# Graph layers on one core: GpSimd's wait for a turn's sums, from group 5 on instead of from group 2 on

## Chip, core and metric

One core of a Trainium2 chip. The metric is the device time of one execution in microseconds, the median of several runs.

## What is computed

12,500 nodes of 32 features, 400,000 edges sorted by destination. Two layers, each followed by a residual and a normalisation:

```python
m = relu(x[src] + edge_attr)
neigh = segment_sum(m, dst)
x = layernorm(x + (1 + eps) * x + neigh)
# second layer
h = x * rsqrt(clip(out_degree, 1))
agg = segment_sum(h[src], dst)
x = layernorm(x + agg * rsqrt(clip(in_degree, 1)))
```

## The kernel before

The edges are cut into 125 groups of 3200 (128 partitions by 25 edges). The first phase, `layer_0`, goes through them in turns, and each engine runs its own program of `step(g, slot, u)`; they meet only in semaphores. `turns` (line 227) writes out g = 0 to 3, runs g = 4 to 119 in a hardware loop of 29 passes by four slots (there `g` is an expression of the loop's register, not a Python integer), and writes out g = 120 to 126.

In turn g these things happen:

- GpSimd (lines 567 to 579) gathers the source nodes' rows of group g from DRAM into `rows`, slot g % 4, by 25 indirect DMAs (`gathers`, line 160), each for 128 edges. Ahead of them it waits for the group's indices (`z_in`), from group 4 on for VectorE's additions of group g - 4 out of the same slot (`z_sum[1]` at g - 3), and for `z_agg` at g - 1.
- VectorE (`step`, line 416) works on the rows of group g - 1: it adds them to the edges' features (`add`, line 426, in two halves; the first waits for all 25 gathers), takes further steps on the sums (`left`, line 431, `last_part`, line 435), and makes one-hot matrices of indices (line 143 records them all). It also makes one-hot matrices (`chunk`) from which TensorE builds, in `built`, counts for the second phase.
- ScalarE copies edge features into the bank (`copy`, line 599), applies the Relu (`first_part`, line 606) and evicts the counts to `stage` (line 621). Its order is written out by hand: the eviction of the first piece stands between `copy(0)` and `first_part(0)`.
- TensorE builds the counts (line 687, 24 matmuls a turn) and sums group g - 1's messages in 25 matmuls (line 667), three each between the last built pieces and 19 at the end. The last one raises `z_agg` to g; "sum g" below is that. So the sum of turn g is that of group g - 1.
- SyncE (line 537) loads, every second turn, the indices and edge features of groups g + 2 and g + 3, behind waits for `z_copy[1]` and `z_idx[3]` at g; it stores each turn's counts to `stash` (line 548). The indices and features of groups 0 to 3 are loaded at the beginning.

After the last turn come `finish_0` (normalisation), `layer_1`, which has no gathers and is TensorE's, and `finish_1`. They follow each other in blocks. `s_mark` is a semaphore that is raised behind waits and that no one waits for.

Of the kernel before, what the change touches and what calls it, by code (L numbers as in the profile page):

```python
# [16 lines left out]
def build(nc, x, src, dst, edge, eps, out, table, x1):  # L17
# [47 lines left out]
    with ExitStack() as ctx:  # L65
# [94 lines left out]
        def gathers(gp, j0, j1, nodes, rows_d, src_d, s):  # L160

            for j in range(j0, j1):
                gp.indirect_dma_start(  # L163
                    rows_d[:, j, :], None, nodes,
                    bass.IndirectOffsetOnAxis(ap=src_d[:, j:j + 1].bitcast(U32), axis=0),
                ).then_inc(s, 16)
# [54 lines left out]
        def layer_0():  # L221
# [5 lines left out]
            def turns(engine, step):  # L227
                for g in range(4):
                    step(g, g, 0)
                with engine.Fori(0, fours) as i:  # L230
                    for slot in range(4):
                        step(i * 4 + (4 + slot), slot, i + 1)
                for g in range(4 + 4 * fours, G + 2):
                    step(g, g % 4, g // 4)

            def builds(g):

                return not isinstance(g, int) or g < G
# [13 lines left out]
            def loaded(engine, s, s_first, slot, use, n):  # L252

                if isinstance(use, int) and use == 1 and slot == 0:
                    engine.wait_ge(s_first, n)
                else:
                    engine.wait_ge(s[slot // 2], use * n)

            with ExitStack() as own:
# [137 lines left out]
                with nc.Block() as block:  # L397
# [163 lines left out]
                    @block.gpsimd  # L561
                    def _(gp):

                        for h in range(2):
                            gp.iota(pick_i[:, h, :], [[1, max(HT)], [0, SPAN]], base=h * HT[0], channel_multiplier=0).then_inc(s_const, 1)

                        def step(g, slot, u):
                            if builds(g):
                                loaded(gp, z_in, z_in0, slot, u + 1, IN)
                                gp.sem_inc(s_mark, 1)  # L570
                                if not isinstance(g, int) or g >= 4:

                                    gp.wait_ge(z_sum[1], g - 3)
                                    gp.sem_inc(s_mark, 1)
                                if not isinstance(g, int) or g >= 2:

                                    gp.wait_ge(z_agg, g - 1)
                                    gp.sem_inc(s_mark, 1)
                                gathers(gp, 0, J, x[:, :], rows[:, slot, :, :], src_t[:, slot, :], z_rows[slot])
                        turns(gp, step)  # L580
# [739 lines left out]
```

## Time and profile before

| | us |
|---|---|
| median of 3 runs (5220.22 to 5222.47) | 5221.61 |
| profiled execution | 5230.44 |
| its span | 5228.60 |
| first phase, to the last gather's start | 3948.04 |
| granted TensorE clock, mean over the span | 0.731 |

```profile
span 5228.6 us, 62768 instructions
...
PE   4555555555555555555555555555555999999997
PEld 1111111111111111111111111111113888888886
DVE  6666666666666666666666666666665444444445
ACT  4555555555555555555555555555554555555553
POOL 6777777777777777777777777777771000000000
```

The digits are the busy share of each engine (PE is TensorE, PEld its weight loads, DVE VectorE, ACT ScalarE, POOL GpSimd) in tenths, in 40 equal slices of the span. The first 30 slices are the first phase, in which POOL is busy, the last nine the second, in which TensorE is. Times below are microseconds from the start of the span.

### The profile page before, as it was taken

Reading aid. Unit: us, or ns where it says so; the run is one execution under the profiler, and the core shown is the slowest. Engines: PE = TensorE matmul, PEld = TensorE weight load, DVE = VectorE, ACT = ScalarE, POOL = GpSimd, SP = SyncE. Lnnn points to the kernel's source line nnn. Section 1 sums busy time; section 2 is a strip of 40 time slices with the busy share of each in tenths; the row PEclk is TensorE's granted clock in tenths of the full one; section 3 lists DMA queues with packets and bytes.
Section 4 is the critical chain, followed back from the end, with each engine's and each line's share of the span. In section 5 each row is a group of like instructions: output and inputs, shape, how many; then the busy total and the mean of one; then the engine's idle time right before and its main releaser. Section 6 shows DMA issues by size and latency. Waiting matters only on the chain. (4 is left out here: it accounts for less than half of the span.)

```text
span 5228.6 us, 62768 instructions
## 1 busy us (share of the span) xinstructions
PE 3323.6 (64%) x21148; PEld 1679.4 (32%) x21148; DVE 3288.0 (63%) x4730; ACT 2760.6 (53%) x2908; POOL 2969.7 (57%) x3134
## 2 busy tenths in 40 slices
PE   4555555555555555555555555555555999999997
PEld 1111111111111111111111111111113888888886
DVE  6666666666666666666666666666665444444445
ACT  4555555555555555555555555555554555555553
POOL 6777777777777777777777777777771000000000
PEclk7666666666666666666666666666666999999998
DMA  3333333333333333333333333333334999999995
GB/s 123 119 119 119 119 130 130 119 119 119 127 133 125 119 119 119 124 136 119 119 119 125 130 130 119 119 119 122 135 119 146 325 324 325 324 325 326 323 324 207
DMA packets 269134, 867.71 MB, mean 166 GB/s; under 512 B 90218, under 2 KB 140218, under 8 KB 252602
## 3 DMA queue, kind: packets, MB, share of 16 engines
q1 hardware_dynamic: 169107, 815.98, 42.1%
q0 software_dynamic: 100000, 51.40, 6.6%
q8 instruction: 13, 0.21, 0.0%
q14 instruction: 14, 0.11, 0.0%
HBM read 486.77 MB, written 380.38 MB: 166 GB/s over the span
## 5 line engine op out<-in xcount | busy, mean ns | idle before, releaser
L163 POOL DMA_INDIRECT rows<-in_x,src_t x3125 | 2968.1, 950 | 976.0 <-issue 946.5
L687 PE MATMUL built<-x_parts,b_hot 100*128 100x490 bf16 x3000 | 1294.1, 535 | 1774.2 <-ACT big L621 1759.8
L621 ACT ACTIVATE big<-built 128x980 bf16<-128x980 f32 x1500 | 1804.4, 1229 | 551.3 <-PE built L687 548.4
L687 PEld LDWEIGHTS built<-x_parts,b_hot 100*128 100x128 bf16 x3000 | 250.1, 111 | 2664.8 <-ACT big L621 2041.7
L426 DVE TENSOR_TENSOR sum_ps<-sum_ps,rows 128x416 f32<-128x416 f32 x250 | 143.0, 572 | 1246.7 <-DMA rows<-in_x,src_t 1242.1
L870 PE MATMUL applied<-counts,x_parts 128*96 128x160 bf16 x12250 | 916.1, 233 | 1.4 <-ACT counts L828 1.4
L667 PE MATMUL agg<-hot,msg 128*128 128x512 bf16 x3125 | 907.2, 441 | 4.9 <-DVE msg L456 4.9
L870 PEld LDWEIGHTS applied<-counts,x_parts 128*96 128x96 bf16 x12250 | 880.2, 123 | 64.9 <-ACT counts L828 2.3
L143 DVE TENSOR_TENSOR x_parts<-iota_ps,hk_g 100x3920 bf16<-100x3920 f16 x375 | 819.6, 2186 | 0.0
L828 ACT ACTIVATE counts<-built 128x980 bf16<-128x980 f32 x500 | 598.8, 1238 | 391.1 <-PE built L856 391.0
L143 DVE TENSOR_TENSOR hot<-iota_ps,s_hi 128x5252 bf16<-128x5252 f16 x250 | 691.4, 2765 | 0.0
L606 ACT ACTIVATE msg<-sum_ps 128x416 bf16<-128x416 f32 x250 | 123.0, 492 | 810.2 <-DVE sum_ps L426 810.2
L667 PEld LDWEIGHTS agg<-hot,msg 128*128 128x128 bf16 x3125 | 352.4, 113 | 510.1 <-issue 248.8
L610 ACT ACTIVATE msg<-sum_ps 128x416 bf16<-128x416 f32 x250 | 126.0, 504 | 387.1 <-DVE sum_ps L431 387.1
L856 PE MATMUL built<-big,hi_hot 100*128 100x490 bf16 x1000 | 273.1, 374 | 33.4 <-DVE big L143 27.8
L143 DVE TENSOR_TENSOR big<-iota_ps,hk_g 100x3920 bf16<-100x3920 f16 x125 | 273.7, 2190 | 0.0
L794 DVE CAST slots<-small 80x64 bf16<-80x64 f32 x125 | 27.6, 221 | 373.0 <-PE small L881 373.0
L143 DVE TENSOR_TENSOR b_hot<-iota_ps,hk_g 100x1024 bf16<-100x1024 f16 x375 | 255.2, 681 | 7.9 <-PE built L687 3.6
L143 DVE TENSOR_TENSOR hot<-iota_ps,rel 128x1404 bf16<-128x1404 f16 x250 | 209.7, 839 | 0.0
L810 DVE TENSOR_TENSOR acc<-acc,small 32x128 f32 x125 | 34.5, 276 | 206.8 <-PE small L891 206.8
L599 ACT ACTIVATE sum_ps<-edge_t 128x416 f32<-128x416 f32 x250 | 127.0, 508 | 67.9 <-DVE msg L435 67.9
L431 DVE SCALAR_TENSOR_TENSOR sum_ps<-sum_ps,msg 128x416 f32<-128x416 f32 x250 | 141.8, 567 | 1.7 <-ACT msg L606 1.7
(130 smaller groups left out, 1452.2 us busy)
## 6 DMA issues: line engine op xcount, KB each, us to landing
stash<-big SPq DMA_DIRECT2D x125, 2940.0 KB, 9.1
counts<-stash SPq DMA_DIRECT2D x250, 1470.0 KB, 8.6
rows<-in_x,src_t POOLq DMA_INDIRECT x3125
edge_t<-in_edge_attr SPq DMA_DIRECT2D x61, 800.0 KB
big<-in_dst SPq DMA_DIRECT2D x1, 1562.5 KB
big<-in_src SPq DMA_DIRECT2D x1, 1562.5 KB
src_t<-in_src SPq DMA_DIRECT2D x61, 24.8 KB
dst_t<-in_dst SPq DMA_DIRECT2D x61, 24.8 KB
```

Of the source, the lines that this page charges most:

```text
L143: return ve.tensor_tensor(out.rearrange("p n (w t) -> p n w t", t=2), row[0:p, 0:w].rearrange("p (w t) -> p w t", t=2).unsqueeze(1).to_bro ...
L163: gp.indirect_dma_start(rows_d[:, j, :], None, nodes, bass.IndirectOffsetOnAxis(ap=src_d[:, j:j + 1].bitcast(U32), axis=0),).then_inc(s, 16)
L426: ve.tensor_tensor(half(h), half(h), rows[:, prev, j0:j1, :], ALU.add).then_inc(z_sum[h], 1)
L431: ve.scalar_tensor_tensor(half(h), half(h), 0.0, part(0, h), ALU.max, ALU.subtract).then_inc(z_left[h], 1)
L599: sc.activation(half(h), edge_t[:, prev, j0:j1, :], ACT.Copy).then_inc(z_copy[h], 1)
L610: sc.activation(part(1, h), half(h), ACT.Copy).then_inc(z_part1[h], 1)
L621: sc.activation(stage[:, slot % 2, q, :, d0:d0 + 2 * SPAN].rearrange("p c (b d) -> p b c d", b=2), built[n % 2][:, :, 0:KEYS].rearrange("p ...
L667: last = te.matmul(agg_bank[:, :], msg[:, j, :], hot[:, j, :], start=(j == 0), stop=(j == J - 1))
L687: last = te.matmul(built[n % 2][:, b, 0:KEYS], b_hot[:, r, t, :], key_hot[:, r, t, :], start=True, stop=True)
L828: sc.activation(counts[:, slot, HB, :, d0:d0 + 2 * SPAN].rearrange("p c (b d) -> p b c d", b=2), built[n % 2][:, :, 0:KEYS].rearrange("p b ...
L856: last = te.matmul(built[n % 2][:, b, 0:KEYS], hi_hot[:, slot, t, :], key_hot[:, slot, t, :], start=True, stop=True)
L870: last = te.matmul(applied[slot].rearrange("m (q d) -> m q d", d=CS), x_parts[:, c, :], counts[:, other, :, c, :], start=(c == 0), stop=(c ...
```

## The change

GpSimd's wait for `z_agg` gets another condition. Where `g` is a Python integer it was there from 2 on and is now there from 5 on. Where `g` belongs to the hardware loop (groups 4 to 119) the condition's first half holds in both versions.

```diff
@@ -572,7 +572,7 @@
                                     gp.wait_ge(z_sum[1], g - 3)
                                     gp.sem_inc(s_mark, 1)
-                                if not isinstance(g, int) or g >= 2:
+                                if not isinstance(g, int) or g >= 5:
 
                                     gp.wait_ge(z_agg, g - 1)
                                     gp.sem_inc(s_mark, 1)
```

## Rows read from the trace of the kernel before

**Rows 1.** The page: busy time of the engines, two of the costliest groups.

```profile
PE 3323.6 (64%) x21148; PEld 1679.4 (32%) x21148; DVE 3288.0 (63%) x4730; ACT 2760.6 (53%) x2908; POOL 2969.7 (57%) x3134
...
L163 POOL DMA_INDIRECT rows<-in_x,src_t x3125 | 2968.1, 950 | 976.0 <-issue 946.5
...
L426 DVE TENSOR_TENSOR sum_ps<-sum_ps,rows 128x416 f32<-128x416 f32 x250 | 143.0, 572 | 1246.7 <-DMA rows<-in_x,src_t 1242.1
```

**Rows 2.** Waits of POOL: total us, times, longest us.

```profile
POOL rows L163 <- issue: 946.5, 3104, 0.3
POOL rows L163 <- PE agg L667: 24.9, 20, 19.1
POOL rows L163 <- DMA dst_t<-in_dst: 4.6, 1, 4.6
```

**Rows 3.** Timeline of POOL: start, duration, instruction, [idle before <- releaser].

```profile
81.17 0.95 POOL L163 DMA_INDIRECT rows<-in_x,src_t  x1 [0.30 <-issue]
101.22 0.95 POOL L163 DMA_INDIRECT rows<-in_x,src_t  x1 [19.10 <-PE agg L667]
...
131.24 0.94 POOL L163 DMA_INDIRECT rows<-in_x,src_t  x1 [0.30 <-issue]
132.49 0.95 POOL L163 DMA_INDIRECT rows<-in_x,src_t  x1 [0.30 <-issue]
...
163.76 0.95 POOL L163 DMA_INDIRECT rows<-in_x,src_t  x1 [0.30 <-issue]
...
195.12 0.95 POOL L163 DMA_INDIRECT rows<-in_x,src_t  x1 [0.31 <-issue]
...
3948.04 0.94 POOL L163 DMA_INDIRECT rows<-in_x,src_t  x1 [0.30 <-issue]
```

**Rows 4.** Line 163, whole span, then 101.2 to 1101.2: ns min/median/max.

```profile
L163 POOL DMA_INDIRECT rows<-in_x,src_t x3125: 943/947/3924, 9.5 to 3948.0; - x196
...
L163 POOL DMA_INDIRECT rows<-in_x,src_t x800: 943/947/1031, 101.2 to 1101.0; - x160
```

**Rows 5.** Timeline of PE: the closing 19 matmuls of sums 1 to 4.

```profile
96.14 4.27 PE L667 MATMUL agg<-hot,msg 128*128 128x512 bf16 x19
...
119.08 4.73 PE L667 MATMUL agg<-hot,msg 128*128 128x512 bf16 x19
...
153.18 4.74 PE L667 MATMUL agg<-hot,msg 128*128 128x512 bf16 x19
...
184.65 4.37 PE L667 MATMUL agg<-hot,msg 128*128 128x512 bf16 x19
```

**Rows 6.** Timeline of DVE: turn 2, turn 3 and the start of turn 4.

```profile
98.13 0.60 DVE L426 TENSOR_TENSOR sum_ps<-sum_ps,rows 128x416 f32<-128x416 f32 x1 [1.02 <-ACT sum_ps L599]
...
102.56 0.60 DVE L431 SCALAR_TENSOR_TENSOR sum_ps<-sum_ps,msg 128x416 f32<-128x416 f32 x1 [1.13 <-ACT msg L606]
...
133.58 0.60 DVE L426 TENSOR_TENSOR sum_ps<-sum_ps,rows 128x416 f32<-128x416 f32 x1 [12.99 <-DMA rows<-in_x,src_t]
...
136.79 0.59 DVE L431 SCALAR_TENSOR_TENSOR sum_ps<-sum_ps,msg 128x416 f32<-128x416 f32 x1
...
165.05 0.60 DVE L426 TENSOR_TENSOR sum_ps<-sum_ps,rows 128x416 f32<-128x416 f32 x1 [10.35 <-DMA rows<-in_x,src_t]
```

**Rows 7.** Timeline of ACT: the copy ahead of turn 3's addition.

```profile
120.47 0.53 ACT L599 ACTIVATE sum_ps<-edge_t 128x416 f32<-128x416 f32 x1
```

**Rows 8.** Timeline before the first turn: two gathers, a VectorE instruction.

```profile
23.46 3.18 POOL L163 DMA_INDIRECT rows<-in_x,src_t  x1 [0.30 <-issue]
...
37.99 3.49 DVE L352 SCALAR_TENSOR_TENSOR big<-x_parts,big 125x3200 f32<-125x3200 f32 x1
...
38.38 3.92 POOL L163 DMA_INDIRECT rows<-in_x,src_t  x1 [0.30 <-issue]
```

**Rows 9.** Timeline of SP's queue: last index load for groups 4 and 5.

```profile
113.58 0.56 SPq L519 DMA_DIRECT2D dst_t<-in_dst  x1
```

**Rows 10.** Timeline of DVE: the last group's first addition.

```profile
3951.02 0.60 DVE L426 TENSOR_TENSOR sum_ps<-sum_ps,rows 128x416 f32<-128x416 f32 x1 [13.24 <-DMA rows<-in_x,src_t]
```

## The prediction

> **What bounds the kernel now.** Read the page first, and its table of engines last. No engine has over 64% of the span, and the page's chain of waits stops after the last microseconds, so neither names the bound. The lines of the costliest groups do [rows 1]: in the first phase VectorE idles 1242.1 us ahead of its additions and was released by the landing of gathered rows, while GpSimd's 976.0 us of idle time is spread over 3125 gathers. The waits view splits that [rows 2]: 946.5 us in 3104 pieces of at most 0.3 us, which end on nothing that the profile shows (the price of starting one gather), and only 24.9 us that ended on TensorE's sums, one piece of them 19.1 us. So in the first phase GpSimd issues gathers one behind another and everything else follows it. One gather costs 1.2508 us from start to start: (131.24 - 101.22) / 24 inside group 2 [rows 3]. A group of 25 costs 31.27 us, which is the distance from group 2's first gather to group 3's, 132.49 - 101.22, and from 3 to 4, 163.76 - 132.49. From group 2 to the end it is the same: (3948.04 - 101.22) / 3074 = 1.2514 us. VectorE takes up the last group's rows 3 us behind the last gather [rows 10], and the rest of the program comes after that in order. What GpSimd gains in the first phase and isn't made to wait for again, the program gains.
>
> **What is removed.** The wait before group g's gathers asks for g - 1 sums. In the diff its start moves from group 2 to group 5, but groups 4 to 119 run in a hardware loop in which g is no Python integer, and there the condition is true in both versions. So exactly two waits go (with one marker increment each), of groups 2 and 3; group 4 keeps its own, for 3 sums. The other waits of groups 2 and 3 (their indices) were met long ago: the indices were among the loads of the beginning.
>
> Group 2. Group 1's last gather starts at 81.17, group 2's first at 101.22 after 19.10 us of idle time [rows 3]; a normal gap is 0.30. Saved: 19.10 - 0.30 = **18.80 us**. New start: 81.17 + 1.25 = 82.42.
>
> Group 3. It followed group 2 without a gap, since sum 2 had come at 119.08 + 4.73 = 123.81 [rows 5], before 132.49. In the new order it starts at 82.42 + 31.27 = 113.69, and now its removed wait matters: kept, it would hold until 123.81 plus the 0.81 us that passed from the end of sum 1 (96.14 + 4.27 = 100.41) to 101.22, so 124.62. Removed, it costs nothing.
>
> The other 19 releases by TensorE in the waits view hold 24.9 - 19.1 = 5.8 us, 0.3 each, the normal gap: nothing is to be had there, and nothing was lost.
>
> **What is next late: group 4.** Its gathers could start at 113.69 + 31.27 = 144.96, if sum 3 is there. Before, sum 3 ended at 153.18 + 4.74 = 157.92 [rows 5], because turn 3 had to wait for group 2's rows. How early can it be now? Turns 0 to 2 use the rows of groups 0 and 1 alone and stay where they were, so sum 2 still ends at 123.81. Group 2's rows now land at about 112.44 + 2.34 = 114.8 (its last gather starts 18.80 us before 131.24; the lag is 133.58 - 131.24 [rows 3, 6]). VectorE isn't ready: it went idle 12.99 us before 133.58, at 120.59 [rows 6], and ScalarE's copy that it adds to ends at 121.00 [rows 7]. So turn 3's first addition starts at 121.1, not at 133.58. It is then a turn with no gap behind the one before, as turn 2 was. There VectorE's next step on the sums (line 431) came at 102.56, 2.15 us after sum 1 ended at 100.41: ScalarE's Relu stands behind an eviction that waits for TensorE, and TensorE was busy with the sum. For turn 3 that gives 123.81 + 2.15 = 125.96. From there to the end of the turn's own sum turn 2 took 123.81 - 102.56 = 21.25 us, turn 3 of before 157.92 - 136.79 = 21.13 [rows 5, 6]. Sum 3: 125.96 + 21.2 = 147.1. Group 4: 147.1 + 0.81 = 147.9. It waits **2.9 us**.
>
> Bounds of that wait. If turn 3 went as a turn with a free TensorE does (turn 4 of before: from 165.05 to 184.65 + 4.37 = 189.02, 23.97 us), sum 3 ends at 121.1 + 23.97 = 145.1, the wait is 0.9. Late end: the 19 closing matmuls took 4.27 to 4.74 us in turns 1 to 4, so the clock of TensorE is worth half a microsecond here; I allow 1.5 for that and for a later eviction, and the wait is 4.4. I take 2.9, since turn 2 is the nearest row: also a turn that starts with no gap, with gathers beside it.
>
> **Behind group 4.** Group 5 could start at 147.9 + 31.27 = 179.2. Turn 4 begins when group 3's rows land, 113.69 + 24 x 1.2508 + 2.34 = 146.05, VectorE being ready at 125.96 + (120.59 - 102.56) = 144.0; sum 4 ends at 146.05 + 23.97 = 170.0, 9 us ahead. From there on each turn waits for its rows as before, where group 5 started at 195.12, 5.3 us behind sum 4's 189.02 plus 0.81: the old steady pattern, not tighter. SyncE's loads of the indices of groups 4 and 5 hang on turn 2, which doesn't move: the last index load was issued at 113.58 [rows 9], 34 us ahead of 147.9 (it was 50). The later loads move with their turns.
>
> **Price of gathers beside other work.** Group 2's gathers now run beside turns 1 and 2 of VectorE, not 2 and 3. Here a row speaks up: at the beginning a gather took 3.92 us instead of 0.95, beside VectorE's float32 instruction over 3200 columns with both inputs in SBUF [rows 8]; there are four such gathers, 3.18 us (the first of them) to 3.92, all beside float32 instructions of VectorE over 3200 columns of SBUF, and 10.1 us over the normal in all. Between 101.2 and 1101.2, 800 gathers beside whole turns, the longest is 1031 ns [rows 4]. The turns hold the same instructions, so I take nothing; the dear end is the same 10.1 us again.
>
> The Trainium skill (SBUF — State Buffer, section "SBUF: two separate sides") says that VectorE and GpSimd share a port pair by an exclusive lock, and that descriptor generation stalls under a two-port VectorE instruction. The four long gathers agree, the 800 don't show it. By that rule a gather that meets one of a turn's small SBUF-only index instructions would be held.
>
> **Sum.** 18.80 - 2.9 = 15.9 us (14.4 to 17.9 by the bounds). The profiled execution of before took 5230.44, its span 5228.60 with 1.84 around it; after: span 5212.7, execution 5214.5. It lies 8.8 us over the median of the runs, 5221.61, in which I subtract the same: **5205.7 us**, 0.30% less. About 0.2% (10.4 us) is what a measurement of this kernel can tell from no change.
>
> **The rivals.** (a) Forecast: -15.9, 5203.7 to 5207.2. Chance 0.62.
> (b) Nothing at group 4: sum 3 comes by 144.1, or group 4 is freed too. All 18.8 us stay: 5202.8. Against it: the shortest turn on record gives 145.1, and the loop's condition doesn't change. Chance 0.14.
> (c) Gathers are held: group 2's or 3's meet VectorE in a way that turns 2 and 3 of before didn't show. With S us of holding the gain is 18.8 less the larger of S and 2.9: at S = 10.1 it is 8.7, 5212.9, within 0.2%; at S = 5 it is 13.8, 5207.8. A late turn 3 or late indices would look alike: over 8.4 us of wait at group 4 end in no change. For it: the four long gathers. Against: 800 gathers without one. Chance 0.20, half of it within 0.2%.
> (d) Slower: the phase between gathers and VectorE's turns shifts for good, and in each of the 121 groups behind group 3 a gather is held under the index instructions. It decides from (15.9 + 10.4) / 121 = 0.22 us a group; one holding as at 23 us, 3.18 - 0.95 = 2.23 us, makes 270 us, 5475 us. Against it: from turn 4 on VectorE starts at the landing of the rows, so gathers and turns stand to each other as before. Chance 0.04.
>
> By the port rule of the Trainium skill (same page and section) (d) would hold wherever a start falls badly; the 1031 ns of [rows 4] bound it at 0.08 us a gather, under the 0.22 a group that decide.
>
> **How the numbers follow.** Faster by over 0.2%: (a), (b) and half of (c), 0.86. Within 0.2%: 0.10. Slower: 0.04. The range goes from (b) less the 1.4 us from the median of the runs to the lowest, 5201.4, to (c) at a holding of about 7.5 us, 5210.5; I leave out the rest of (c) and (d).
>
> **What the profile after would show.** GpSimd: no gap at 81 us, group 2's first gather at 82.4 and group 3's at 113.7, one gap of about 3 us ahead of group 4's at 147.9, released by TensorE's sum; group 5 near 179.2; the last gather at 3932.1. VectorE: turn 2 unmoved at 98.13, turn 3's addition at 121.1, turn 4's at 146. SyncE: index loads still at 108 to 114. The second phase has its old length. Wrong would be the forecast by a gap of over 4.4 us at group 4, by gathers over 1.1 us after 50 us, by a step from start to start other than 1.251 us in the loop, or by a gap inside it.

## The result, and the profile after

| | before | after |
|---|---|---|
| median, us | 5221.51 (8 runs, 5219.81 to 5222.47) | 5206.22 (8 runs, 5204.13 to 5206.82) |
| profiled execution, its span | 5230.44, 5228.60 | 5206.82, 5205.00 |

The changed kernel takes 0.9970 of the time (95% interval 0.9961 to 0.9979), 15.3 us less; the forecast was 5205.7, 15.9 less. That holds on the chip of this comparison and on two others (0.9969 and 0.9967). On a further chip the same change costs 28 us, which the section on experiments comes to.

The page of after (as [rows 1]):

```profile
span 5205.0 us, 62766 instructions
...
L163 POOL DMA_INDIRECT rows<-in_x,src_t x3125 | 2959.4, 947 | 961.7 <-issue 947.2
```

and its waits of GpSimd (as [rows 2]):

```profile
POOL rows L163 <- issue: 947.2, 3108, 0.3
POOL rows L163 <- PE agg L667: 10.2, 16, 5.6
```

Against [rows 2] the piece of 19.1 us is gone, and a new one of 5.6 us has come. The timeline of GpSimd says where (start, duration, [idle before <- releaser]; the answer to [rows 3]):

```profile
79.83 0.94 POOL L163 DMA_INDIRECT rows<-in_x,src_t  x1 [0.30 <-issue]
81.08 0.94 POOL L163 DMA_INDIRECT rows<-in_x,src_t  x1 [0.30 <-issue]
...
112.28 0.94 POOL L163 DMA_INDIRECT rows<-in_x,src_t  x1 [0.30 <-issue]
...
142.24 0.94 POOL L163 DMA_INDIRECT rows<-in_x,src_t  x1 [0.30 <-issue]
148.79 0.94 POOL L163 DMA_INDIRECT rows<-in_x,src_t  x1 [5.61 <-PE agg L667]
...
180.02 0.95 POOL L163 DMA_INDIRECT rows<-in_x,src_t  x1 [0.30 <-issue]
...
3925.09 0.94 POOL L163 DMA_INDIRECT rows<-in_x,src_t  x1 [0.30 <-issue]
```

Group 2 starts at 81.08, group 3 at 112.28, both without a gap. Group 4 waits 5.6 us for sum 3 and starts at 148.79, 14.97 us ahead of the 163.76 of before. Nothing waits after it. TensorE's closing matmuls of sums 2 to 4 in after (the answer to [rows 5]):

```profile
119.35 4.85 PE L667 MATMUL agg<-hot,msg 128*128 128x512 bf16 x19
...
143.03 4.96 PE L667 MATMUL agg<-hot,msg 128*128 128x512 bf16 x19
...
165.84 4.26 PE L667 MATMUL agg<-hot,msg 128*128 128x512 bf16 x19
```

VectorE in turn 3 and at the start of turn 4 (the answer to [rows 6]); turn 3 is 12.2 us ahead of before and follows turn 2 with 0.3 us of idle time:

```profile
121.37 0.60 DVE L426 TENSOR_TENSOR sum_ps<-sum_ps,rows 128x416 f32<-128x416 f32 x1 [0.30 <-ACT sum_ps L599]
...
126.35 0.60 DVE L431 SCALAR_TENSOR_TENSOR sum_ps<-sum_ps,msg 128x416 f32<-128x416 f32 x1 [1.68 <-ACT msg L606]
...
144.98 0.60 DVE L426 TENSOR_TENSOR sum_ps<-sum_ps,rows 128x416 f32<-128x416 f32 x1 [0.18 <-ACT sum_ps L599]
```

The spans of the two profiles differ by 23.6 us, not by 15. Of that 14.97 lie ahead of group 4 and 7.98 behind it: there the gathers step by (3925.09 - 148.79) / 3024 = 1.2488 us in this profile and by 1.2514 in that of before. The medians give 15.3, and the profiled execution of before lay 8.9 us over its median, that of after 0.6, so I put the 8 us down to that one execution of before: at its pace the median would lie near 5230 too. The pace isn't tied to the program either. The kernel without the wait (below) has a median gather of 0.944 us on chip 0 and of 0.947 on chip 10. But both profiles of before show 0.947 and all four of the changed kernel 0.944, and no second profile of before on a chip of this kind was taken, so this stays argued.

### The profile page after: what moved, and what is told of

Same layout as the page of the kernel before. It is cut to its first block and busy times, and to the rows that moved or that the text cites. A ratio compares the mean times of both kernels' runs of the same rounds, so it can differ in the third digit from the quotient of the medians.

```text
span 5205.0 us, 62766 instructions
## 1 busy us (share of the span) xinstructions
PE 3317.5 (64%) x21148; PEld 1678.5 (32%) x21148; DVE 3284.0 (63%) x4730; ACT 2758.7 (53%) x2908; POOL 2961.1 (57%) x3134
```

## The experiments

### Which gaps are left: no wait for sums at all

The changed kernel twice more, and a kernel without the wait in any group:

```diff
-                                if not isinstance(g, int) or g >= 2:
-
-                                    gp.wait_ge(z_agg, g - 1)
-                                    gp.sem_inc(s_mark, 1)
```

> The changed kernel, unchanged, beside the kernel before. In the runs so far the kernel before takes 5221.5 us in one set and 5861.1 in the other, where TensorE's sums end some 14 us later in every turn while its recorded matmuls are no longer. If this set is like the first: 5206.2 against 5221.5, ratio 0.997. If it is like the second, the first theory (one head start of 15.9 us, then a steady state that doesn't know how it began) gives 0.997 again; the rival, by which gathers that run beside a sum hold TensorE back, gives a changed kernel that is slower than before by up to 20 us, as dropping group 2's wait alone (+13.3) and group 3's alone (+19.9) were there.

> The kernel without the wait for sums in any group, which took 6774.8 us in the set in which the kernel before takes 5861. Theory: two kinds of chip. On the first (before at 5221.5) TensorE isn't held back beside gathers, and the only thing left to be had is the gap ahead of group 4, 4 to 5 us in the profiles: 5201 to 5202. On the second it repeats 6775. Rival: the wait in the loop is needed on the first chip as well: over 5210.

> The changed kernel in the same set, for comparison. On the first kind of chip 5206, 0.997 of before. On the second kind: if the steady state doesn't know how it began, 15 to 20 us less than 5861; if gathers started ahead meet the sums for good, 5875 to 5885, as with either wait of the two dropped alone.

Measured: the first after, on chip 5, 5205.68 (before 5221.91, ratio 0.9969, 0.9956 to 0.9981). On chip 0, in one set: before 5221.65, after 5205.18 (0.9967, 0.9955 to 0.9980), without the wait 5202.42 (0.9963, 0.9949 to 0.9977). GpSimd's timeline at group 4's first gather, after on chip 5:

```profile
148.35 0.94 POOL L163 DMA_INDIRECT rows<-in_x,src_t  x1 [4.15 <-PE agg L667]
```

after on chip 0:

```profile
148.18 0.94 POOL L163 DMA_INDIRECT rows<-in_x,src_t  x1 [3.97 <-PE agg L667]
```

and without the wait on chip 0, with the last gather of all:

```profile
144.78 0.94 POOL L163 DMA_INDIRECT rows<-in_x,src_t  x1 [0.30 <-issue]
...
3921.30 0.94 POOL L163 DMA_INDIRECT rows<-in_x,src_t  x1 [0.30 <-issue]
```

The gap of 3.7 to 3.9 us over the normal accounts for the difference to the kernel without the wait (3.4 us at group 4 on chip 0, 2.8 in the medians), and in that kernel GpSimd has no gap behind the first gather. So on these chips the wait holds nothing but group 2 before and group 4 after, and 19.2 us (5221.65 - 5202.42) is all that it costs before.

### GpSimd as the bound: 13 of 25 gathers

```diff
-                                gathers(gp, 0, J, x[:, :], ...)
+                                gathers(gp, 0, 13, x[:, :], ...)
```

with VectorE's wait for the rows lowered to match; the rows of the other 12 edges are zeros.

> The changed kernel with 13 of a group's 25 gathers; the rows of the other 12 edges of each partition are zeros, so that part of the gathering is left out. Where the kernel before takes 5221.6: GpSimd needs 13 x 1.249 = 16.2 us a turn and is no longer the bound; the next one is VectorE's turn with no gap, 23.5 us (98.36 to 121.37 to 144.98 in the profile after), so the time falls by 122 x 7.7 = 940 us, to 4270. If something else than GpSimd set the pace, it falls by less than 400. Where the kernel before takes 5850 to 5861: if TensorE is held only while gathers run, the 16.2 us of gathers leave it free for the rest of a turn and the turn falls from 36.2 us to under 28 (below 4880 in all); if its sums are late for another reason, the 36.2 us stay and the time with them, 5880.

Measured, on chip 2: 4215.87 against 5222.03 (ratio 0.8074, 0.8061 to 0.8088). The time falls with the gathers until something else sets the pace. The closing matmuls of four sums in the loop:

```profile
1016.99 4.93 PE L668 MATMUL agg<-hot,msg 128*128 128x512 bf16 x19
...
1039.78 4.27 PE L668 MATMUL agg<-hot,msg 128*128 128x512 bf16 x19
...
1062.69 4.28 PE L668 MATMUL agg<-hot,msg 128*128 128x512 bf16 x19
...
1085.63 4.75 PE L668 MATMUL agg<-hot,msg 128*128 128x512 bf16 x19
```

GpSimd's waits for the sums (total, times, longest):

```profile
POOL rows L163 <- PE agg L668: 910.1, 121, 55.8
```

A turn now takes 22.8 us from sum to sum, (1090.38 - 1021.92) / 3, about the 22.5 to 23.6 of a VectorE turn with no gap in the profiles before and after (over the whole loop it is 23.0). GpSimd idles (910.1 - 55.8) / 120 = 7.1 us ahead of a group. (I had said 4270, with 23.5 us a turn.) At 25 gathers it is GpSimd's 31.2 us that count, as the prediction had it.

### Another kind of chip

The first set of runs fell on chip 10. It held the kernel before once more, the two waits one at a time, and the kernel without the wait:

```diff
-                                if not isinstance(g, int) or g >= 2:
+                                if not isinstance(g, int) or g >= 3:
```
```diff
-                                if not isinstance(g, int) or g >= 2:
+                                if not isinstance(g, int) or g == 2 or g >= 4:
```

> The kernel before, unchanged, for a second profile of it. The profile after shows 1.2488 us from gather to gather in the loop, (3925.09 - 148.79) / 3024, the profile of before 1.2514, (3948.04 - 163.76) / 3024. If that pace belongs to the execution and not to the change, this profile may show 1.249 as well, with the gap ahead of group 2 still there: group 2's first gather at 101 us, a span near 5220. If the change made GpSimd faster, the pace stays at 1.2514 and the span at 5228. Time 5221.5 either way.

> Group 2's wait goes, group 3's stays (condition from 3 on). By the accounting of the prediction sum 2 ends at 124.2, as in the profile after (119.35 + 4.85), so group 3's gathers start at 125.0 instead of 112.3, a gap of about 12.7 us; group 4 starts at 125.0 + 31.2 = 156.2, with no gap, since sum 3 (148.0) is there. The gain over before is that of group 4's start, 163.6 - 156.2 = 7.4 us: 5214.1. Rival: the two waits are worth the same or only the first counts: 15 us, 5206.2.

> Group 3's wait goes, group 2's stays. Group 3's wait was met 8 us before it was asked for, so nothing changes: 5221.5, gap ahead of group 2 as in before. Rival: the wait or its marker costs time of its own, so that dropping it gains some tenths of a microsecond.

> The wait for sums is gone in every group, those of the loop too; the wait for VectorE's additions of four groups back stays. If only the gap ahead of group 4 (5.3 us in the profile after) was left to be had, group 4 starts at 143.5 and the time is 5.3 us under the changed kernel: 5200.9, between it and 5203.5 if the gap is as small in other executions as I had forecast (2.9). Gaps in the loop: none in either. Rival: the wait in the loop paces the gathers usefully, and without it they meet something else; then the time is over 5206.

A later set fell on chip 11, with the first of these two and the changed kernel:

> Group 2's wait goes, group 3's stays; in the slower set this was 13.3 us over before. On a chip where the kernel before takes 5221.6: sum 2 ends at 124, so group 3's gathers start at 124.6 to 125.0, 12.5 us after they could; group 4 follows 31.2 us later, at 156, with no gap; 163.6 - 156 = 7.5 us are kept: 5214.1. Rival (only group 2's wait counts): 5206.

> The changed kernel in the same set. Where before takes 5221.6: 5206. Where before takes 5861: see the expectation of the third such run, 5845 if the head start is all, 5875 to 5885 if gathers started ahead meet the sums for good.

On chip 10 nothing came as expected. On chip 11 the changed kernel came inside the 5875 to 5885 that I had given for gathers that meet the sums for good. On these chips the kernel before itself takes 5861.1 and 5850.9 us:

| chip, kernel | median | over before of its set | group 4 starts at |
|---|---|---|---|
| 10, before | 5862.9 | 1.8 | 203.17 |
| 10, only group 2's wait dropped | 5874.4 | 13.3 | 215.9 |
| 10, only group 3's wait dropped | 5881.0 | 19.9 | 223.38 |
| 10, no wait | 6774.8 | 913.6 | 197.8 |
| 11, only group 2's wait dropped | 5861.8 | 10.9 | 217.1 |
| 11, after | 5879.1 | 28.2 | 232.59 |

GpSimd's timeline at the starts of groups 2, 3 and 4, kernel before on chip 10:

```profile
130.92 0.95 POOL L163 DMA_INDIRECT rows<-in_x,src_t  x1 [49.04 <-PE agg L667]
...
167.04 0.94 POOL L163 DMA_INDIRECT rows<-in_x,src_t  x1 [5.17 <-remote]
...
203.17 0.94 POOL L163 DMA_INDIRECT rows<-in_x,src_t  x1 [5.18 <-remote]
```

and at the start of group 4, after on chip 11:

```profile
232.59 0.94 POOL L163 DMA_INDIRECT rows<-in_x,src_t  x1 [88.11 <-PE agg L667]
```

Here the wait for the sum ends last in every group, not only in the second (5.2 us idle, 4.9 over the normal gap; "remote" is a release of which the profile has no record). The period of a group is 36.2 us on chip 10 and 36.1 on chip 11 in every kernel of the table that keeps the wait in the loop, whatever its start. What differs is where group 4 stands, and that difference is carried to the end: 12.7, 20.2 and 29.4 us at group 4 against 13.3, 19.9 and 28.2 in the medians (the last pair crosses from chip 10 to chip 11; within chip 11 its two kernels are 15.5 us apart at group 4 and 17.3 in the medians). So the first half of my theory stands there too: the steady state doesn't know how it began. The other half, that gathers started earlier cost nothing, doesn't.

Why are the sums late? Three timelines of one turn of the kernel before on chip 10. ScalarE:

```profile
1015.49 1.20 ACT L621 ACTIVATE big<-built 128x980 bf16<-128x980 f32 x1 [0.89 <-PE built L687]
1024.40 1.26 ACT L621 ACTIVATE big<-built 128x980 bf16<-128x980 f32 x1 [7.71 <-issue]
```

TensorE's closing matmuls, and the second piece of the next turn, which stands behind them in its program:

```profile
1017.16 4.26 PE L667 MATMUL agg<-hot,msg 128*128 128x512 bf16 x19
...
1025.71 1.00 PE L687 MATMUL built<-x_parts,b_hot 100*128 100x490 bf16 x2 [3.87 <-issue]
```

GpSimd, the last gather of a group and the first of the next:

```profile
1029.77 0.94 POOL L163 DMA_INDIRECT rows<-in_x,src_t  x1 [0.30 <-issue]
1035.84 0.95 POOL L163 DMA_INDIRECT rows<-in_x,src_t  x1 [5.13 <-remote]
```

ScalarE's second line is the eviction of a piece that TensorE's record has done at 1017.3; it starts 7 us later. The 19 closing matmuls are recorded as over at 1021.42, but GpSimd, which waits for them, is let go at about 1035.84 - 0.81 = 1035.0, 4.3 us after the last gather ended. So the release comes some 14 us after the end of the record (12.9 in the median of 100 turns, 9.3 to 14.5; 0.01 in the profile of before that the prediction rests on), and 4.4 us after the last gather in the median. One record per turn is missing (3000 of 3125 of line 667).

Are the matmuls late, or only the news of them? The traces also keep the times at which semaphores were raised. At the end of this sum `z_agg` was raised at 1035.05, and `z_built` of the next turn's first two pieces, whose matmuls stand behind the sum, at 1035.09 and 1035.13. In the median of the 100 turns the three come within 0.09 us. In the profile of before on the other kind of chip they lie 0.42 and 0.84 us apart, which is the time that the pieces' matmuls take. Work of 0.84 us isn't done in 0.09, so on chip 10 these pieces were done before the news of them came, and it came all at once. The record of the second piece says so too: it starts at 1025.71, 9 us ahead of the release of the sum in front of it. So no row shows late matmuls there; what the rows show late is TensorE's raising of semaphores, and what waits on it is late in turn.

The beginning shows the same with no turn around it, in ScalarE's copies of TensorE's transposes. In the profile of before that the prediction rests on, 14 of them take 9.2 us:

```profile
47.92 9.16 ACT L586 ACTIVATE hk_all<-built 100x500 f16<-100x500 f32 x14 [0.33 <-PE built L381]
```

On chip 10 the same kernel's last four end on ever longer waits:

```profile
60.85 0.59 ACT L586 ACTIVATE hk_all<-built 100x500 f16<-100x500 f32 x1 [2.26 <-PE built L381]
65.80 0.59 ACT L586 ACTIVATE hk_all<-built 100x500 f16<-100x500 f32 x1 [4.35 <-remote]
72.84 0.59 ACT L586 ACTIVATE hk_all<-built 100x500 f16<-100x500 f32 x1 [6.46 <-remote]
83.34 0.59 ACT L586 ACTIVATE hk_all<-built 100x500 f16<-100x500 f32 x1 [9.91 <-remote]
```

There the gathers of groups 0 and 1 ran until 81.9; the last copy comes at 83.34 and TensorE then goes at its usual rate. The first nine copies come at the usual pace, though gathers run beside them, and then the waits grow. In the turn above the gathers resume at 999.75 and the evictions are on time until 1015.49. So it isn't that each instruction is slower beside a gather; the lateness builds up while gathers run on without a long pause. In after on chip 11 gathers ran on through groups 2 and 3, until 145, and the evictions of turn 0 came 4.9 to 6.3 us apart until then instead of 1.2: turn 1 began at 161.6, on chip 10 in before at 106.7. That is what makes the change dear there, as I read it: 62.5 us more of gathers before the first pause, and a start of group 4 that is 29 us later. The second phase, which has no gathers, is as fast as elsewhere: TensorE is busy for 1174.6 of 1200 us between 4650 and 5850.

The Trainium skill (Perfetto Trace Analysis, "Summary: the profiler window per engine type") says that the reported end of a TensorE instruction is an estimate, and that the way of a semaphore from there isn't in the profile. Records that end 7 and 14 us before what waits on them don't contradict it. Which of the two is late, the matmul or its semaphore, the page doesn't say; the times above do.

Why TensorE's semaphores come late beside gathers on chips 10 and 11, and not on 0, 2 and 5, stays open. All that the runs show is the coincidence in time, in three places (the beginning, the end of each turn's sum, and the kernel without the wait, in which gathers pause only where the next indices aren't loaded yet, and a group takes 43.5 us). Two other causes would be late transfers and late loads of instructions. Against the first, a gather's last packet ends 2.1 us after the gather's start in the median on both kinds of chip. Against the second, the two queues of instruction loads carry 13 and 14 packets in the profiles of before on either, too few for over 100 late turns. The run with 13 gathers was meant to tell more, but fell on a chip of the first kind. Each chip was seen in one set of runs only, so that it is the chip, and not something else about the set, is argued too.

### What a held gather costs

```diff
+                            if not isinstance(g, int):
+                                for part_ in range(3):
+                                    ve.scalar_tensor_tensor(extra[:, part_, :, :], extra_in[:, 0:1, :]..., 1.0,
+                                                            extra_in[:, 1:2, :]..., ALU.mult, ALU.add)
```

at the end of a turn in the changed kernel; in the second kernel `iota_bank[:, 0:100]...` in PSUM takes the place of `extra_in[:, 1:2, :]`.

> The changed kernel with three more VectorE instructions in every turn of the loop, scalar_tensor_tensor over 900 float32 columns with both inputs in SBUF, some 0.95 us each, put where VectorE then waits some 10 us for rows. They are no part of the computation. If such an instruction holds a gather (the rule of the port lock, rival d), each of 116 turns loses about what the three take together, up to 2.9 us, and never under 0.5: 5206 + 60 to 330. If the long gathers of the beginning have another cause: within 1 us of 5206, since VectorE's own idle time covers them.

> The same three instructions, but the second input is read from PSUM. If it is the two inputs in SBUF that hold gathers, as the 800 undisturbed gathers beside one-hot instructions with an input in PSUM say: within 1 us of 5206. If any long float32 instruction of VectorE does it: as slow as with both in SBUF.

Measured on chip 11, where after takes 5879.08: 5818.33 with both inputs in SBUF (ratio to before 0.9941, 0.9925 to 0.9958), 5877.61 with one in PSUM (1.0044, 1.0028 to 1.0061). The timeline with both inputs in SBUF, a gather and the three instructions beside it:

```profile
1035.04 5.14 POOL L163 DMA_INDIRECT rows<-in_x,src_t  x1 [0.30 <-issue]
1036.27 3.10 DVE L510 SCALAR_TENSOR_TENSOR extra<-extra_in 128x900 bf16<-128x900 f32 x3
```

The timeline with one input in PSUM, the same:

```profile
1013.13 3.08 DVE L510 SCALAR_TENSOR_TENSOR extra<-extra_in,iota_ps 128x900 bf16<-128x900 f32 x3
1013.47 0.94 POOL L163 DMA_INDIRECT rows<-in_x,src_t  x1 [0.30 <-issue]
1014.71 0.94 POOL L163 DMA_INDIRECT rows<-in_x,src_t  x1 [0.30 <-issue]
```

All gathers of the two kernels (ns min/median/max), SBUF first:

```profile
L163 POOL DMA_INDIRECT rows<-in_x,src_t x3125: 942/947/5971, 9.5 to 4540.9; - x196
```

```profile
L163 POOL DMA_INDIRECT rows<-in_x,src_t x3125: 938/944/4233, 9.2 to 4595.3; - x196
```

The control came as expected: with an input in PSUM the time is that of after, and behind group 3 no gather takes over 1.05 us (the 4233 is one of the beginning). With both inputs in SBUF the gathers behind group 3 take 513 us more in all (3367.5 against 2854.6), 4.4 us in each of the loop's 116 turns, beyond the 2.9 I had as the most. So the rule of the Trainium skill (SBUF — State Buffer, "SBUF: two separate sides"), an exclusive lock between the two engines, agrees with these rows. The time went the other way from what I expected, since on this chip GpSimd had 4.9 us of waiting a group to give: that gap is gone (0.02 us is left), and a group takes 35.6 instead of 36.1 us. The last gather starts at 4540.9 instead of 4596.8, 55.9 us earlier; the medians differ by 60.8. Here the sums' releases are in time again (0.02 us after the end of the record in the median, 12.8 in the changed kernel on the same chip): a gather that is held for 5 us late in the turn does what the pause between two groups does. What the lock would cost where GpSimd is the bound was not measured; 4.4 us x 116 = 510 us is an estimate from this run.

## Why the prediction was right, and where it wasn't

**The bound** was read rightly: GpSimd's gathers, 31.2 us a group. With 13 of 25 left the kernel is 1006 us below before, and the loop has no gap.

**Group 2** starts at 81.08, forecast 82.42. The head start comes as said; the rest is the profile of after itself, whose first 50 gathers were 1.3 us quicker (a first start 0.3 earlier, and the held ones of the beginning).

**Group 3's wait** had to go as well for the gain. Sum 2 ended at 119.35 + 4.85 = 124.20, 11.9 us after group 3's start. The run that was to price this on its own fell on the other kind of chip both times, so on this kind it rests on these two rows.

**The gap ahead of group 4** is the term that was mis-sized: 2.9 forecast, bounds 0.9 to 4.4; the profiles show 5.3, 3.9 and 3.7. A gap of over 4.4 us was one of the prediction's own signs of being wrong, and it came in the first of the three; so did another, a step other than 1.251 us in the loop (1.2488, see above). Two terms of it missed. Turn 3 began at 121.37 (121.1), its step on the sums at 126.35 (125.96), and sum 3 ended at 147.99 (147.1), 0.9 late: 0.4 of it was there in sum 2, the rest is the 21.6 us from that step to the sum, against 21.2. And group 3's last gather was over earlier, so that group 4 could have started at 143.49 instead of 144.96: a faster GpSimd waits the longer, for the sum doesn't move. The start of group 4 is the better number, and it was 148.79 against 147.9. The rival that nothing is left at group 4 (b) is out; the loop's condition holds for group 4, as read from the diff.

**Behind group 4**: sum 4 at 170.10 (170.0), group 5 at 180.02 (179.2), no gap in the loop. Group 3's rows were no longer what turn 4 waited for (forecast 146.05 for its start, measured 144.98, released by ScalarE), which changed nothing.

**Held gathers** (c): none outside the beginning, as the 800 gathers of [rows 4] said. The four long ones there are not all as the prediction has them: the first (23.46) stood beside an instruction with int32 inputs (line 343), the second (34.45) beside two with a single input (lines 350 and 351); all of them read only SBUF. The experiment shows that they would be held by another kind of VectorE instruction.

**The slower side** (d) was given 0.04, and its mechanism, a phase that shifts for good, was seen on no chip. Slower did happen, on chip 11, by a mechanism that no row of before could show: TensorE's semaphores late beside gathers. The step that failed there is "turns 0 to 2 use the rows of groups 0 and 1 alone and stay where they were": with the change turn 1 began at 161.6 us on chip 11, without it at 106.7 on chip 10.

**The sum**: 15.9 us forecast; 15.3, 16.2 and 16.5 in three comparisons. That the comparison fell on a chip of this kind was luck: on chip 11 the same forecast, 5835, is 44 us off.

## What to carry to other kernels

A wait that is dropped in a prologue is worth the distance between two starts, that of the next wait in the same chain before and after; follow the chain to the first wait that stays, since it takes back what the engine got too early. A steady state that an engine's own rate sets keeps such a head start and doesn't multiply it (15.0 us at group 4, 15.3 in the medians). Time such a change on more than one chip: a wait that is idle on one was the pace on another, and there its removal from the loop cost 15.6%.

## What the runs showed of the hardware

- The same program takes 5221 to 5222 us on chips 0, 2 and 5 and 5851 to 5863 on chips 10 and 11. All but 4 us of the difference of the spans, 629 of 633, is there at the last gather (4576.9 against 3948.0), and TensorE's sums are released 9.3 to 14.5 us after the end of their records (0.01 on the other chip), together with the two pieces behind them, within 0.09 us in the median.
- A gather of 128 rows takes GpSimd 0.944 or 0.947 us, by the median of each profile, and 0.30 to the next, on all chips; beside three VectorE instructions of 3.10 us in all with both float32 inputs in SBUF one took 5.14 us, beside the same with an input in PSUM 0.95.
